# Where the last down product and the turn stand in each step of a graph-attention kernel

## What is computed

```python
h = relu(layernorm(x))
for l in range(3):                        # first network, with self loops
    s = leaky(si[:, None] + sj[None, :] + attn_b[l])      # si, sj = h @ attn_w
    h1 = layernorm(h + softmax(where(mask, s, -inf)) @ h) * g1 + beta1
    h = layernorm(h1 + gelu(h1 @ W1[l] + b1) @ W2[l] + b2) * g2 + beta2
x = x + h
h = relu(layernorm(x))                    # second network, one layer
Wh = h @ W
e = where(adj > 0, leaky(Wh @ a1 [:, None] + Wh @ a2 [None, :]), -9e15)
x = x + leaky(softmax(e, axis=1) @ Wh)
```

## Time and profile before

| | |
|---|---|
| median of 3 runs | 2058.97 us (2058.65 to 2061.35) |
| the profiled execution's own time | 2060.88 us |
| its span, first to last instruction | 2059.1 us |
| busy: PE, DVE, ACT, POOL | 92%, 76%, 61%, 43% of the span |
| mean granted TensorE clock | 0.987 of full speed |
| chain that ended last | PE 44%, DVE 35%, POOL 8%, ACT 7%, issue 5% |

### The profile page before, as it was taken

How to read it: one execution, slowest core, us unless ns; L and a number is a source line. 1 busy time by engine, 2 the same in 40 slices (tenths; PEclk the granted TensorE clock), 3 DMA queues, 4 the chain that set the end, 5 groups by cost and what they waited for, 6 DMA issues and landing times.

```text
span 2059.1 us, 30847 instructions
## 1 busy us (share of the span) xinstructions
PE 1884.9 (92%) x11009; PEld 1588.0 (77%) x11009; DVE 1556.0 (76%) x4920; ACT 1252.4 (61%) x1948; POOL 879.6 (43%) x703
## 2 busy tenths in 40 slices
PE   3899999999999989999899999999989999899995
PEld 2787877887787878778778787787877788778884
DVE  6677887688776797768877688667886678776755
ACT  2565656666656566675566665757656666566662
POOL 3355453435433444343534354433453435433450
PEclk9999999999999999999999999999999999999998
DMA  4001100011000110001100011000100011000100
GB/s 164 21 32 36 47 11 21 1 42 37 6 21 1 42 42 1 21 1 47 36 1 21 11 37 36 1 21 21 52 11 17 5 42 32 11 12 1 32 1 21
DMA packets 40625, 52.33 MB, mean 25 GB/s; under 512 B 2926, under 2 KB 30872, under 8 KB 40472
## 3 DMA queue, kind: packets, MB, share of 16 engines
q1 hardware_dynamic: 40472, 50.37, 7.7%
HBM read 41.97 MB, written 8.39 MB: 24 GB/s over the span
## 4 chain that ended last, share of the span: by engine, by line
PE 44%; DVE 35%; POOL 8%; ACT 7%; issue 5%; DMA 0%; DVEq 0%; POOLq 0%; ACTq 0%
PE acc L423 12%; PE acc L490 11%; PE ps_u L462 7%; PE acc L527 5%; DVE probs L917 5%; POOL columns L1234 4%; PE acc L509 3%; DVE probs L1046 2%; DVE stats L977 2%; DVE probs L1050 2%; POOL probs L1274 2%; DVE junk L885 2%; DVE stats L831 2%; DVE normed L949 2%; PE ps_t L386 1%
## 5 line engine op out<-in xcount | busy, mean ns | idle before, releaser
L490 PE MATMUL acc<-w_hi,gelu_hi 128*128 128x256 f32 x1536 | 469.1, 305 | 12.7 <-DVE gelu_lo L967 7.5
L706 ACT ACTIVATE g_full<-ps_u,vec_all 128x512 f32<-128x512 f32 x384 | 259.2, 688 | 339.3 <-PE ps_u L462 172.0
L423 PE MATMUL acc<-x_nat,probs 128*128 128x257 f32 x1536 | 387.6, 401 | 52.2 <-ACT probs L681 26.8
L490 PE MATMUL acc<-w_hi,gelu_lo 128*128 128x256 f32 x1536 | 433.7, 282 | 0.0
L490 PE MATMUL acc<-w_lo,gelu_hi 128*128 128x256 f32 x1536 | 433.0, 282 | 0.0
L1268 POOL TENSOR_TENSOR gelu_lo<-g_full,gelu_hi 128x512 fp32r<-128x512 f32 x240 | 310.5, 1302 | 284.2 <-ACT gelu_hi L714 225.0
L423 PEld LDWEIGHTS acc<-x_nat,probs 128*128 128x128 f32 x1536 | 283.5, 195 | 154.0 <-ACT probs L681 52.2
L1234 POOL TENSOR_TENSOR columns<-columns 128x4 f32<-128x4 f32 x128 | 135.8, 1061 | 560.6 <-DVE columns L846 560.6
L490 PEld LDWEIGHTS acc<-w_hi,gelu_hi 128*128 128x128 f32 x1536 | 292.2, 190 | 27.0 <-POOL gelu_lo L1268 11.1
L490 PEld LDWEIGHTS acc<-w_lo,gelu_hi 128*128 128x128 f32 x1536 | 292.8, 191 | 5.4
L490 PEld LDWEIGHTS acc<-w_hi,gelu_lo 128*128 128x128 f32 x1536 | 290.9, 189 | 0.0
(11 more groups left out here) (128 smaller groups left out, 3590.5 us busy)
## 6 DMA issues: line engine op xcount, KB each, us to landing
adj_in<-adj_dram SPq DMA_DIRECT2D x64, 256.0 KB, 2.7
x_nat<-x_dram SPq DMA_DIRECT2D x16, 512.0 KB, 5.4
x_res<-x_dram SPq DMA_DIRECT2D x16, 512.0 KB, 4.3
out_dram<-x_res SPq DMA_DIRECT2D x64, 128.0 KB, 1.7
x_res<-L_gnn_W_dram SPq DMA_DIRECT2D x5, 1024.0 KB, 5.4
mask_g<-L_gnn_W_dram SPq DMA_DIRECT2D x1, 1024.0 KB, 12.5
attn_row<-L_gnn_attn_w_dram SPq DMA_DIRECT2D x1, 512.0 KB
g_row<-L_gnn_g_dram SPq DMA_DIRECT2D x1, 384.0 KB
```

The lines of the kernel that those rows point to most:

```text
L423: last = pe.matmul(acc[side][c % 2][:, 0:D + 1], probs[:, j, c * P:(c + 1) * P], x_nat[:, side, j, :], start=(j == 0), stop=(j == NC - 1))
L490: last = pe.matmul(acc[side][c // 2][:, cols:cols + D], h[:, r, tok], w[:, layer, f, :], start=False, stop=(f == FC - 1 and i == 2), skip_ ...
L706: full = act.activation(g_full[:, f % 2, :], ps_u[f % 2][:, :], ACT.Gelu, bias=b1_col[:, layer, f:f + 1])
```

## The change

On TensorE, in every step but the first of all, the last down product of step n - 1 moves behind the high half of step n's first up products (`up_first_high`, `down(n - 1, ..., 7)`, `up_first_low`). The turn moves behind down 6. The residual of a second node block moves ahead of up 2 (in steps 0 and 5 that of the first one). In steps 1 and 3 down 2 and the scores row stand before the final output; in step 2 the bound rows before down 2. The last wait for the copies of wh moves behind up 6.

On ScalarE, the exponentials of the second network's first two chunks move from the end of steps 0 and 2 to behind gelu 2 of the next step. In step 2 the low row and the copy of the turned h come before gelu 4. On VectorE, in steps 1 and 3 gelu_high comes ahead of the statistics, gelu_lo 1 right after them, and both scalings behind the scores; h_lo is made in the middle of the final scores or of the layer scores; in step 5 gelu_lo 3 comes first; the diagonal of the kept mask of side 1 moves from step 5 to step 0 of the next pair, with its four columns copied aside. On GpSimd, in steps 1 and 3 gelu_lo 0 comes before the inverse root.

```diff
+        diag_kept = vec_all[:, VECS + 2 * LAYERS:VECS + 2 * LAYERS + NC]
...
+                self.takes_down = not self.begins
+                self.leaves_down = self.attend
...
@@ TensorE: start_of
-                up_first(n, layer)
+                up_first_high(n, layer)
+                if s.takes_down:
+                    down(n - 1, s.other, layer if side == 1 else (layer - 1) % LAYERS, 7)
+                up_first_low(n, layer)
                 pe.wait_ge(h_act.sem, h_act.at(n))
                 soon = s.attend and s.layer_a == 0 and not s.begins
                 if soon:
                     scores_row(n + 1)
-                else:
-                    residual(n, side, 0)
+                if s.masks_in is not None:
+                    pe.wait_ge(mask_ready.sem, mask_ready.at(s.masks_in, 2))
+                residual(n, side, 0)
+                if not soon:
+                    residual(n, side, 1)
...
@@ TensorE: slot
                 if s.late is not None:
+                    down(n, side, layer, 2)
+                    scores_row(n + 1)
                     final_out(s.late[0], free, (0, 1), n - 1)
-                if s.late is not None:
-                    scores_row(n + 1)
                     final_out(s.late[0], free, (2, 3))
...
-                if soon:
+                if soon or early_turn:
                     bound_rows(n + 1)
-                down(n, side, layer, 2)
+                if s.late is None:
+                    down(n, side, layer, 2)
...
+                if s.final is not None:
+                    pe.wait_ge(wh_copy.sem, wh_copy.at(s.final[0]))
                 attend_out(n + 1, other, s.layer_a, graph_a)
...
                 down(n, side, layer, 5)
+                down(n, side, layer, 6)
                 pe.wait_ge(q_ready.sem, q_ready.at(n + 1))
                 turn_tokens(normed, ln1_apply, h_tr, n + 1, ps_t)
-                down(n, side, layer, 6)
                 if s.prepare is not None:
                     mask_transposes(s.prepare, side, free)
-                down(n, side, layer, 7)
+                if not s.leaves_down:
+                    down(n, side, layer, 7)
...
@@ ScalarE
                     gelu(n, layer, 2)
+                    if s.late is not None:
+                        final_exps(s.late[0], (0, 1))
...
                     gelu(n, layer, 3)
+                    early_turn = s.final is not None and s.layer_a > 0
+                    if early_turn:
+                        low_row(n + 1)
+                        final_h(s.final[0], free)
                     gelu(n, layer, 4)
...
                     h_split(n + 1, s.layer_a)
-                    if s.final is not None:
-                        final_exps(s.final[0], (0, 1))
...
@@ VectorE: ff_norm
+                if late is not None:
+                    gelu_high(n + 1)
                 for c in range(NC):
...
                 variance(ln2_chain, n)
-                if follows:
+                if follows and late is None:
                     gelu_high(n + 1)
                 if late is not None:
-                    final_scale(late, 0)
+                    gelu_rest(n + 1, 1)
...
                 half(1)
-                if late is not None:
-                    final_scale(late, 1)
...
+                if late is not None:
+                    final_scale(late, 0)
+                    final_scale(late, 1)
...
@@ VectorE: final_bounded
-                if step is not None:
-                    h_rest(*step)
+                    if step is not None and j == 1:
+                        h_rest(*step)
...
@@ VectorE: pair_body
+                        gelu_rest(n, 3)
                         if s.prepare is not None and s.side == 1:
-                            final_mask(pair * 2 + 1, 1)
                             prepare_masks(s.prepare, 1, (0,))
-                        gelu_rest(n, 3)
...
+                    if s.side == 0 and s.layer == 0 and not first:
+                        final_mask(pair * 2 - 1, 1, diag_kept)
...
@@ GpSimd
+                    if s.late is not None:
+                        gelu_rest(n, 0)
                     if not s.begins:
                         inverse_root(ln2_chain, n - 1, ln2_rstd)
-                    gelu_rest(n, 0)
+                    if s.late is None:
+                        gelu_rest(n, 0)
```

More of the change, by code:

```diff
@@ L551, in start_of @@
                     scores_row(n + 1)
-                else:
-                    residual(n, side, 0)
+                if s.masks_in is not None:
[3 more added lines that the diff above has]
+                    residual(n, side, 1)
                 up(n, layer, 2)
                 up(n, layer, 3)
-                down(n, side, layer, 0, s.late[0] if s.late is not None else None, s.masks_in, (0,) if not soon else ())
+                down(n, side, layer, 0, s.late[0] if s.late is not None else None, s.masks_in, (0,) if soon else (0, 1))
                 down(n, side, layer, 1)
@@ L581, in slot @@
                 up(n, layer, 5)
-                if not soon:
+                if not soon and not early_turn:
                     bound_rows(n + 1)
@@ L792, in pair_body @@
                         continue
-                    if s.final is not None and s.layer_a > 0:
-                        final_h(s.final[0], free)
+                    if early_turn:
                         final_wh(s.final[0], free)
-                    low_row(n + 1)
+                    else:
+                        low_row(n + 1)
                     if s.final is not None and s.layer_a == 0:
@@ L869, in input_shift, with token_dots @@
                                          op0=ALU.mult, op1=ALU.mult).then_inc(ln0_shift.sem, 1)
-            def token_dots(source, row_i, row_j, init_i, init_j, to_i, to_j):
-                for c in range(NC):
+            def token_dots(source, row_i, row_j, init_i, init_j, to_i, to_j, chunks):
+                for c in chunks:
                     dve.tensor_tensor_reduce(junk[:, 2 * c * D:(2 * c + 1) * D], source(c), row_i, 1.0, init_i,
@@ L1002, in ff_norm @@
                 half(0)
-                if follows and scores is not None:
+                if follows and scores is not None and late is None:
                     gelu_rest(n + 1, 1)
                 half(1)
-                if late is not None:
-                    final_scale(late, 1)
                 if follows and scores is None:
@@ L1015, in ff_norm, with layer_scores @@
                     dve.wait_ge(s_ready.sem, s_ready.at(step_next))
-            def layer_scores(n, side, g):
+                if late is not None:
+                    final_scale(late, 0)
+                    final_scale(late, 1)
+            def layer_scores(n, side, g, step=None):
                 dve.wait_ge(x0_ready.sem, x0_ready.at(g))
-                token_dots(lambda c: x_nat[:, side, c, 0:D], attn_row[:, 0, 0, :], attn_row[:, 0, 1, :],
-                           bias_col[:, 0, 0:1], 0.0, s_i, s_j).then_inc(s_ready.sem, 1)
+                for chunks in ((0, 1), (2, 3)):
+                    last = token_dots(lambda c: x_nat[:, side, c, 0:D], attn_row[:, 0, 0, :], attn_row[:, 0, 1, :],
+                                      bias_col[:, 0, 0:1], 0.0, s_i, s_j, chunks)
+                    if step is not None and chunks == (0, 1):
+                        h_rest(*step)
+                last.then_inc(s_ready.sem, 1)
                 dve.wait_ge(s_ready.sem, s_ready.at(n))
@@ L1166, in pair_body @@
                     else:
+                        gelu_rest(n, 3)
                         if s.prepare is not None and s.side == 1:
-                            final_mask(pair * 2 + 1, 1)
                             prepare_masks(s.prepare, 1, (0,))
-                        gelu_rest(n, 3)
-                    if s.layer_a > 0 or s.begins:
+                    rows_first = s.final is not None or (s.layer_a == 0 and not s.begins)
+                    if not rows_first:
                         gelu_rest(n, 4)
                     bounded_scores(n + 1, other, s.late[0] if s.late is not None else None)
-                    if s.layer_a == 0 and not s.begins:
+                    if rows_first:
                         gelu_rest(n, 4)
+                    if s.side == 0 and s.layer == 0 and not first:
+                        final_mask(pair * 2 - 1, 1, diag_kept)
                     if first and s.side == 0 and s.layer + 1 < LAYERS:
@@ L1182, in pair_body @@
                     if s.side == 1 and s.layer == 1:
-                        final_mask(pair * 2, 0)
+                        final_mask(pair * 2, 0, diag_mask[:, 0, :])
+                        if not last:
+                            dve.tensor_copy(diag_kept, diag_mask[:, 1, :])
                     if s.early_masks is not None:
@@ L1201, in pair_body @@
                         final_bounded(s.final[0], s.final[1], free, (n + 1, s.layer_a))
-                    else:
+                    elif s.prepare is None:
```

19 lines of the change are left out of this document (13 added, 6 removed).

## The result

| | before | after |
|---|---|---|
| median of 4 runs | 2060.05 us (2058.65 to 2061.35) | 2092.55 us (2091.39 to 2099.46) |
| ratio, 95% interval | | 1.0168 (1.0155 to 1.0181) |
| profiled execution: own time, span | 2060.88, 2059.1 us | 2099.46, 2097.7 us |

The changed kernel is slower by 32.5 us, 1.7%. The forecast was 2054 us with a range of 2036 to 2070 us: sign, size and range were wrong.

The account below looks back on a forecast made before the run. TensorE in six middle pairs, short of work only in small gaps, beside a dependence loop of similar length. Steps summed to -0.7 us a pair, -4 for six; with -1.2 in the first, -5: 2054 us, range 2036 to 2070.

Parts of the forecast that it names:

- boundary: Passage between steps, turn behind down 6 and down 7 between the halves: 1.5 us more, 0.6 where mask transposes follow.
- None or one such meeting: Steps 1 and 3: VectorE's wh scaling and shift meeting GpSimd's products cost 0 to 1.3 us, taken as 0.5.
- Slower, at step 1 and 3: Rival: scaling and shift meet GpSimd's products each time; 2065 us, above 2080 for two meetings, centre 2068; chance 0.24.
- scaling over 1 us in steps 1 and 3: Sign that the prediction is wrong: VectorE's shift or scaling of wh takes over 1 us there.
- 1.5 - 0.33 - 0.4 (small starts): +0.7 us: Step 4: boundary price less 0.33 and 0.4 us of smaller TensorE gaps, so 0.7 us slower.
- The later end of down 7: Down 7 done 0.9 us before the low half ends, not 2.8: nothing in steps 2 and 4, 0.5 us if uncovered.
- The rest of step 2: Step 2 beside the boundary: 1.8 us of projection gaps go, bounds wait some 1.2 us; whole step -0.9 us.
- step 4's wait for the norm: Step 4's turn waited 0.97 us for the norm; down 6 covers it, but the lead is lost again.
- Idle ahead of the high half: Sign of being right: TensorE idle about 0.9 and 0.3 us before the high half, released by h_hi, in 46 steps.
- Step 5: Held by VectorE; moving the kept mask's diagonal to step 0 saves 1.0 us.
- The 0.7 us that the prediction worked out from it: Step 5: if gelu_lo 3 is held to the end of GpSimd's product, the saving is 0.7 us a pair, not 1.1.
- Step 2's forecast wait for the bounds: Step 2: row bounds ahead of down 2 come late from VectorE, so TensorE waits some 1.2 us.

Follow-up runs that it names:

- e2: Changed kernel with the old order in all steps: turn before down 6, down 7 before the high half; 2055.33 us.
- e5: Changed kernel with the old boundary in all steps and GpSimd's products in steps 1 and 3 waiting for the scaling of wh; 2020.23 us.
- e1: Changed kernel, but GpSimd starts its products for x_nat in steps 1 and 3 only when the scaling of wh is done; 2069.34 us.
- e6: Kernel before with only the turn moved behind down 6, down 7 still ahead of the high half; 2105.17 us.
- e7: Kernel before with only down 7 moved between the halves of the up products, the turn still ahead of down 6; 2070.38 us.
- e8: e5 with down 7 between the halves of the up products in all steps, the turn still ahead of down 6; 2033.99 us.
- e11: e5 with gelu_lo 3 ahead of the last two leaky chunks on VectorE in steps 1 and 3; 2021.48 us.

## Why the prediction was wrong

What each step of a middle pair gave, in us, by the stretches above. The third line is e2, the change without its boundary; the last is e5. In the pair taken here step 5 holds a stretch of lower granted clock in all four kernels (0.96 on the mean of the step), which costs it 1.1 us (39.9 against 38.8 in other pairs), and every other step stands at 1.00.

| step | 1 | 2 | 3 | 4 | 5 | 0 | sum |
|---|---|---|---|---|---|---|---|
| forecast | +0.3 | -0.9 | +0.1 | +0.7 | -1.0 | +0.1 | -0.7 |
| after less before | +1.83 | -0.07 | +1.84 | +1.41 | -1.18 | +0.55 | +4.4 |
| e2 less before | +0.87 | -2.00 | +0.86 | -0.29 | -1.15 | -0.03 | -1.7 |
| e5 less before | -1.03 | -2.00 | -1.02 | -0.29 | -1.14 | -0.04 | -5.5 |

**The step that failed first** is "None or one such meeting: 0 to 1.3 us; I take 0.5, since the scaling itself never took over 0.36 us in 64 instructions". The meeting came in every step 1 and 3, twice each, and made two pairs of 0.62 us into 2.59 and 2.33 us: 3.7 us of VectorE, of which 1.9 lay on the path (e1). The 64 rows of 352 ns came from a place where none of GpSimd's products of 128x512 ran beside them. 28 of them lie beside its inverse root on 4 elements a partition, which did not hold them, and 14 start 0.01 us before the end of a product. So they said nothing of a meeting with such a product; the rows that did were counted for one meeting at most. And a TENSOR_SCALAR with one tensor in had met one in the same trace. From the kernel before, the scaling beside the inverse root, then step 5:

```profile
1079.45 1.12 POOL L1234 TENSOR_TENSOR columns<-columns 128x4 f32<-128x4 f32 x1 [8.12 <-DVE columns L846]
1079.81 0.62 DVE L1082 TENSOR_SCALAR wh<-wh,columns 128x256 f32<-128x256 f32 x2
...
1251.40 1.26 POOL L1244 TENSOR_TENSOR normed<-normed,g_row 128x512 f32<-128x512 f32 x1
1251.45 1.24 DVE L898 TENSOR_SCALAR columns<-s_both 128x4 f32<-128x4 f32 x1
```

The rival "Slower, at step 1 and 3" had the mechanism and its place, and for two meetings "above 2080"; the sign of being wrong, "scaling over 1 us in steps 1 and 3", came. It deserved most of the chance. Without the meeting step 1 and 3 together stand at -0.1 us in e1 against a forecast of +0.4 less the 1.0 allowed for the meeting, -0.6: close, by terms that partly cancel.

**The second** is the boundary in steps 2 and 4. Its price of 1.5 us was near what the late turn alone takes (e6, 1.5 and 1.0 us), but it was priced as TensorE's gap ahead of the high half, and so other gaps of TensorE were set against it: "1.5 - 0.33 - 0.4 (small starts): +0.7 us" in step 4, 1.5 - 0.33 in step 2. After less e2 gives what it took: 1.93 us in step 2 and 1.70 in step 4. The later end of down 7, which the prediction put "at nothing" in these two steps, is part of it: 0.7 us in step 2 and 0.2 to 0.3 in step 4 (e7, e8). The rest of step 2 was right (-2.0 us; the forecast's -0.9 less 1.17 is -2.1). e6 has no gap ahead of the high half at all and costs 46 us: the turn starts a chain (h_hi, h_last, h_lo, statistics, scores; or h_hi, exponentials, two table loads, first gelu) whose length from the turn stays the same however TensorE fills its time, so a shorter gap of TensorE pays for none of it. In steps 1 and 3 that chain is out of the way in the changed kernel, and the boundary takes 0.96 us of the 1.5. That a turn behind down 6 hides step 4's wait for the norm was right, and worth nothing, since the norm's wait was for that chain too.

The miss of 5.1 us a pair (+4.4 for -0.7) is then, in three parts: the meeting took 3.8 us for the 1.0 allowed (2.8); the boundary 6.1 for the 6.6 in the sum (-0.5); and the savings, e5 less before, were 5.5 us for the 8.3 that the prediction's terms make when both costs are taken out (2.8). Of these 2.8 us, steps 1 and 3 lack 0.7 and 0.9, steps 2, 4 and 0 lack 0.4 to 0.5 each, and step 5 has 0.1 to spare. Such a sum takes each gap of TensorE as time on the path, and e11 shows one that is not; the gaps of step 1 also add up to 2.6 us by the prediction's own terms, where it has 2.7. What each gap was worth stays open. Seven such pairs make 36 us, near the 38.5 us between forecast and median. That the changed kernel without its boundary (e2) has a median of 2055.33 us, a microsecond from the forecast for the whole, is luck.

**What held.** Idle ahead of the high half: 0.76 us printed and released by h_hi, 0.9 forecast, and a second one shorter. Step 5: -1.18 us for -1.0. VectorE's and GpSimd's rows around gelu_lo 3 in step 5 of after:

```profile
1269.98 1.27 POOL L1277 TENSOR_TENSOR normed<-normed,g_row 128x512 f32<-128x512 f32 x1
1270.03 1.24 DVE L920 TENSOR_SCALAR columns<-s_both 128x4 f32<-128x4 f32 x1
1271.19 0.16 DVE L921 TENSOR_SCALAR columns<-s_both 128x4 f32<-128x4 f32 x1
1271.26 0.68 DVE L989 TENSOR_TENSOR gelu_lo<-g_full,gelu_hi 128x512 fp32r<-128x512 f32 x1
1271.33 1.76 POOL L1283 TENSOR_TENSOR x_res<-x_res,normed 128x512 f32<-128x512 f32 x1
1271.86 1.51 DVE L875 TENSOR_SCALAR mask_nat<-adj_in 128x512 bf16<-128x512 int32 x1
```

gelu_lo 3 came 0.07 us ahead of the product and was not held; the product took 1.76 us for its usual 1.3, and the mask instruction behind took 1.51 us for a median of 0.43 and ended 0.28 us after the product. That is the order of issue of the Trainium skill's section, with the other engine first. The 0.7 us that the prediction worked out from it for the opposite order did not come, and its own spoke against that order: the mask's first instruction, whose place gelu_lo 3 took, was 0.07 us ahead of the product too (1252.67 and 1252.74). The first pair lost nothing (313.33 us to the first attention product of step 0, 313.39 before). The waits for gelu 0 (14.1 us in the run) and around the projection (7.5 us for h_last, of which 1.2 are left, and 6.6 for the last wh) are gone from TensorE in e5. Step 2's forecast wait for the bounds is there (1.49 us); down 3's also, at no cost (e11).

The range failed because its slow end took half of a rival whose own price was above 2080 us for two meetings, and because nothing in it allowed the boundary to cost in full while the savings fell short.

What stays open: in which steps the lower clock falls, and why. The profiled run of after, 7 us above its median, had a granted clock of 0.984 where its other runs had 0.988. Its last stretch is 265.7 us for 257.2 before; 5.1 of these 8.5 us lie in steps 1 to 4 of the last pair, as in every pair, and the rest was not taken apart. And the boundary's 0.96 us in steps 1 and 3 has a mechanism that fits, but no run of its own.

## What to carry to other kernels

An instruction's duration from a place where no other engine works beside it says nothing of a place where one does: when a change moves it next to a run of products on another engine, price it with the longest meeting in the trace, whatever the kind, or order the two by a wait, which here cost nothing that the runs show and gave back 3.8 us a pair, 23 us of the changed kernel. An instruction that starts a chain over several engines belongs as early as its input allows, even if the engine that issues it has other work to fill the time: measure the distance from it to the last instruction of the chain, and if that is the same in two kernels and the chain is what the step waits for, each us of lateness is paid in full. And read the granted clock beside each time: here a difference of 0.008 in its mean went with 17 us between runs of one kernel (e2), more than several of the effects that were looked for.

## What the runs showed of the hardware

A VectorE TENSOR_SCALAR on float32 with one SBUF tensor in and one out, 128x256, took 352 ns alone and up to 1440 ns while GpSimd ran TENSOR_TENSOR on 128x512; I had given that little chance. Beside GpSimd's TENSOR_TENSOR on 4 elements a partition (1.12 us, 1079.45 in the kernel before) two of them took their usual 0.62 us. A TENSOR_SCALAR on 4 elements a partition took 1.24 us in the company of such a product (1270.03) and 0.16 right after it (1271.19), so that a small instruction was held as long as a large one. The wait that keeps the two engines apart adds nothing to GpSimd's own products: 1.29, 1.27, 1.28 and 1.09 us in e1, and 1.30, 1.28, 1.32 and 1.09 us in the changed kernel.
